# Gated cross-attention and ternary feed-forward layer: four of six bias products issued as 32-row tiles

## What is computed

```python
def bit_linear(x, w, b):                       # x rounded to 255 levels per token, w to -1, 0, 1
    gamma_x = clip(max(abs(x), axis=-1), 1e-05); scale_x = 127.0 / gamma_x
    x_dq = clip(round(x * scale_x), -128, 127) / scale_x
    gamma_w = clip(mean(abs(w)), 1e-05)
    w_dq = clip(round(w / gamma_w), -1, 1) * gamma_w
    return x_dq @ w_dq.T + b
x = x + tanh(g_xattn) * attention(layernorm(x), ctx)
h = layernorm(x)
x = x + tanh(g_ffn) * bit_linear(silu(bit_linear(h, gate_w, gate_b)) * bit_linear(h, val_w, val_b), out_w, out_b)
```

## Time and profile before

| | us |
|---|---|
| median of 3 runs | 773.2 (772.61 to 775.05) |
| profiled execution | 772.76 |
| its span, first to last instruction | 771.0 |
| TensorE products busy | 706.6 |
| VectorE busy | 622.7 |
| ScalarE busy | 535.4 |
| GpSimd busy | 316.9 |

### The profile page before, as it was taken

One profiled execution on the slowest core, in us unless ns is written; L12 is line 12 of the kernel. 1 busy time (PEld: TensorE's weight loads), 2 busy tenths in 40 slices (PEclk: granted clock), 3 DMA queues, 4 the chain that ended last, 5 costly groups with the idle time before them and its releaser, 6 DMA issues.

```text
span 771.0 us, 13495 instructions
## 1 busy us (share of the span) xinstructions
PE 706.6 (92%) x4204; PEld 341.1 (44%) x4253; DVE 622.7 (81%) x1290; ACT 535.4 (69%) x701; POOL 316.9 (41%) x482
## 2 busy tenths in 40 slices
PE   4989755878999999999999999999999999999997
PEld 3434434433544454445444444444444544454443
DVE  6868797697778987798779877987798778778885
ACT  4575778977657956786678856795588657856554
POOL 4310315223554356344643454346444553354440
PEclk9999886989999999999999999999999999999999
DMA  9864426121453354435443354326433542244312
GB/s 324 254 232 124 116 83 212 42 39 45 113 130 67 83 111 105 106 82 109 95 116 82 80 124 90 85 63 129 106 79 81 115 96 62 55 93 86 83 42 69
DMA packets 177386, 81.07 MB, mean 105 GB/s; under 512 B 156595, under 2 KB 156851, under 8 KB 176710
## 3 DMA queue, kind: packets, MB, share of 16 engines
q1 hardware_dynamic: 177350, 80.62, 42.7%
HBM read 38.75 MB, written 10.51 MB: 64 GB/s over the span
## 4 chain that ended last, share of the span: by engine, by line
PE 37%; DVE 33%; issue 10%; ACT 6%; DMA 5%; another core or an unknown queue 5%; POOL 2%; SPq 1%; DVEq 0%; POOLq 0%; ACTq 0%
PE psum L1739 12%; PE psum L1705 11%; PE psum L1730 5%; DVE psum L1227 3%; DVE hmax L1240 2%; DMA arena<-x_both 2%; PE psum L1709 2%; DVE arena L1235 2%; PE psum L1932 2%; ACT arena L921 2%; DVE xmax L1312 2%; DVE stats L1300 2%; DVE arena L1346 2%; DVE stats L1266 2%
## 5 line engine op out<-in xcount | busy, mean ns | idle before, releaser
L1705 PE MATMUL psum<-ternary,xqT 128*128 128x512 f16 x1024 | 259.6, 382 | 3.2 <-DVE xqT L1257 1.1
L1705 PEld LDWEIGHTS psum<-ternary,xqT 128*128 128x128 f16 x1024 | 98.3, 98 | 120.3 <-DVE arena L1232 2.8
L665 POOL TENSOR_TENSOR rstd<-var_e,minus_half 128x1 f32<-128x1 f32 x64 | 39.8, 623 | 211.1 <-DVE var_e L1304 111.1
L1730 PE MATMUL psum<-ternary,arena 128*128 128x512 f16 x496 | 121.7, 379 | 1.5 <-DMA arena<-arena 1.5
L855 ACT ACTIVATE arena<-psum,dequant 128x512 f32<-128x512 f32 x128 | 87.1, 681 | 49.7 <-PE psum L1709 47.4
L1739 PE MATMUL psum<-wo_hi,arena 128*128 128x512 f16 x256 | 82.6, 384 | 0.3
L1240 DVE TENSOR_REDUCE hmax<-arena 128x1 f32<-128x1024 f32 x64 | 77.6, 1213 | 0.8
L1739 PE MATMUL psum<-arena,wq_hi 128*128 128x512 f16 x256 | 76.1, 379 | 1.7 <-DMA arena<-x_both 1.1
L863 ACT ACTIVATE arena<-arena,round_c,hscale 128x1024 f32<-128x1024 f32 x62 | 73.5, 1235 | 1.9 <-DVE hscale L1252 1.9
L895 ACT ACTIVATE arena<-arena,round_c 128x1024 f16<-128x1024 f32 x62 | 70.8, 1142 | 0.3
L1730 PEld LDWEIGHTS psum<-ternary,arena 128*128 128x128 f16 x496 | 46.2, 98 | 54.8 <-issue 3.8
(11 more groups left out here) (213 smaller groups left out, 1302.1 us busy)
## 6 DMA issues: line engine op xcount, KB each, us to landing
arena<-in_x SPq DMA_DIRECT2D x64, 256.0 KB, 2.8
out<-arena SPq DMA_DIRECT2D x31, 256.0 KB, 2.4
arena<-in_L_ffn_gate_w SPq DMA_DIRECT2D x4, 1024.0 KB, 12.9
arena<-in_L_ffn_out_w SPq DMA_DIRECT2D x3, 1024.0 KB, 4.9
ternary<-in_L_ffn_val_w SPq DMA_DIRECT2D x2, 1024.0 KB, 11.9
kcur<-k_scratch SPq DMA_DIRECT2D x56, 32.0 KB, 2.2
arena<-arena SPq DMA_TRANSPOSE x90, 3.1
ternary<-in_ctx SPq DMA_DIRECT2D x1, 1024.0 KB, 5.4
```

What stands on the lines that cost most here:

```text
L1705: ins = M.matmul(ps[:], xqT[:, t % 2, k, :], w[:, k, cols], start=(k == 0), stop=(k == KC - 1 and not biased))
L1730: ins = M.matmul(psO[:], hidT[t % 2][:, k, :], wo2[:, k, :], start=(k == 0), stop=(k == FC - 1))
```

## The change

The first product of a tile's block 0 is now preceded by four products of 32 rows each: rows 0 to 31 of inv_rows and bias_parts into psG[0], rows 32 to 63 into psG[1], rows 64 to 95 into psV[0], rows 96 to 127 into psV[1]. They open the sums of gate and value blocks 0 and 1, and the eight products of those blocks add to them. Gate blocks 2 and 3 keep a full bias product of 128 rows (the three other groups are zero there). Value blocks 2 and 3 get theirs from VectorE, value blocks 0 and 1 no longer do. Ahead of the four, TensorE waits until the readers of block 3 of the tile before are done (not for t = 0). For the four groups the inverse scale's parts are repeated four times, and the biases are stored three times to a larger scratch, so that the rows are read back in five DMAs.

```diff
-        bias_dram = nc.dram_tensor("bias_scratch", [PARTS, 2, F], BF16, kind="Internal").ap()
+        bias_dram = nc.dram_tensor("bias_scratch", [PARTS, PARTS, 2, F], BF16, kind="Internal").ap()
-        bias_parts = sb("bias_parts", [P, F + F // 2], BF16)
+        bias_parts = sb("bias_parts", [P, 3 * CW], BF16)
-        ones_p = sb("ones_p", [P, 2, PARTS])
+        ones_p = sb("ones_p", [P, 2, 2, PARTS])
+        BIAS_ROWS = [(2 * g + h, 0, g, slice(h * CW, (h + 1) * CW)) for g in range(2) for h in range(2)]
+        BIAS_ROWS += [(0, 1, 0, slice(2 * CW, 4 * CW))]
-                    sp.dma_start(valb_b[:, :], bcast(val_b[0:F // 2], F // 2)).then_inc(s_vbias, 16)
+                    sp.dma_start(valb_b[:, :], bcast(val_b[F // 2:], F // 2)).then_inc(s_vbias, 16)
-            sp.dma_start(bias_dram.rearrange("j g (p c) -> p (j g) c", p=P),
-                         bias_cut.rearrange("p j g c -> p (j g) c")).then_inc(s_bst, 16)
+            for r in range(PARTS):
+                sp.dma_start(bias_dram[r].rearrange("j g (p c) -> p (j g) c", p=P),
+                             bias_cut.rearrange("p j g c -> p (j g) c")).then_inc(s_bst, 16)
-            sp.wait_ge(s_bst, 16)
-            for i in range(2 * PARTS):
-                g, j = i // PARTS, i % PARTS
-                n = F // 2 if g else F
-                sp.dma_start(bias_parts[PARTS * i:PARTS * (i + 1), g * F:g * F + n],
-                             bias_dram[j:j + 1, g, F - n:].to_broadcast([PARTS, n])).then_inc(s_brow, 16)
+            sp.wait_ge(s_bst, 16 * PARTS)
+            for r, at, g, cols in BIAS_ROWS:
+                sp.dma_start(bias_parts[GROUP * r:GROUP * r + PARTS * PARTS, at * CW:at * CW + cols.stop - cols.start],
+                             bias_dram[:, :, g, cols].rearrange("r j n -> (r j) n")).then_inc(s_brow, 16)
-                parts = inv_cols[:, t % 2, 0:2 * PARTS * PARTS].rearrange("p (g i j) -> p g i j", g=2, j=PARTS)
+                parts = inv_cols[:, t % 2, :].rearrange("p (g h n) -> p g h n", g=2, h=2)
-                    G.tensor_tensor(parts[:, :, :, j], ones_p[:],
-                                    src.rearrange("p (g a) -> p g a", a=1).to_broadcast([P, 2, PARTS]),
-                                    ALU.mult).then_inc(iv_part.sem, 1)
+                    G.tensor_tensor(parts[:, :, :, PARTS * j:PARTS * (j + 1)], ones_p[:],
+                                    src.rearrange("p (g a n) -> p g a n", a=1, n=1)
+                                    .to_broadcast([P, 2, 2, PARTS]), ALU.mult).then_inc(iv_part.sem, 1)
-                    if n < BIASED_BY_VECTOR:
+                    m = n - (NCH - BIASED_BY_VECTOR)
+                    if m >= 0:
+                    if i == 0 and t:
+                        wait(pe, silu_done, b, m - 1)
+                        wait(pe, hid_ready, b, m - 1)
+                    if i == 0:
+                        for r in range(4):
+                            part = slice(GROUP * r, GROUP * (r + 1))
+                            M.matmul((psG, psV)[r // 2][r % 2][:], inv_rows[part, t % 2, :], bias_parts[part, 0:CW],
+                                     start=True, stop=False)
-                        if m > 2:
+                        if i >= 2:
                             wait(pe, used, b, m - 2)
+                        last_bias = g == 0 and i >= 2
                         for k in range(KC):
-                            biased = g == 0 or i >= BIASED_BY_VECTOR
-                            ins = M.matmul(ps[:], xqT[:, t % 2, k, :], w[:, k, cols], start=(k == 0),
-                                           stop=(k == KC - 1 and not biased))
-                        if biased:
-                            at = (g * F // 2) + i * CW
-                            ins = M.matmul(ps[:], inv_rows[:, t % 2, :], bias_parts[:, at:at + CW],
+                            ins = M.matmul(ps[:], xqT[:, t % 2, k, :], w[:, k, cols], start=(i >= 2 and k == 0),
+                                           stop=(k == KC - 1 and not last_bias))
+                        if last_bias:
+                            ins = M.matmul(ps[:], inv_rows[:, t % 2, :], bias_parts[:, (i - 1) * CW:i * CW],
                                            start=False, stop=True)
```

More of the change, by code:

```diff
@@ L687, in update_inverse @@
                     src = left if j else whole
-                    G.tensor_tensor(parts[:, :, :, j], ones_p[:],
-                                    src.rearrange("p (g a) -> p g a", a=1).to_broadcast([P, 2, PARTS]),
-                                    ALU.mult).then_inc(iv_part.sem, 1)
+                    G.tensor_tensor(parts[:, :, :, PARTS * j:PARTS * (j + 1)], ones_p[:],
+                                    src.rearrange("p (g a n) -> p g a n", a=1, n=1)
+                                    .to_broadcast([P, 2, 2, PARTS]), ALU.mult).then_inc(iv_part.sem, 1)
                     if j < PARTS - 1:
                         wait(pool, iv_part, row, PARTS * t + j + 1)
-                        G.tensor_tensor(left, src, parts[:, :, 0, j], ALU.subtract).then_inc(iv_left.sem, 1)
+                        G.tensor_tensor(left, src, parts[:, :, 0, PARTS * j], ALU.subtract).then_inc(iv_left.sem, 1)
                         wait(pool, iv_left, row, (PARTS - 1) * t + j + 1)
@@ L1223, in hidden @@
                     wait(dve, v_done, b, NCH * t + n + 1)
-                    if n < BIASED_BY_VECTOR:
-                        if not prev and (t, n) == (0, 0):
+                    m = n - (NCH - BIASED_BY_VECTOR)
+                    if m >= 0:
+                        if not prev and (t, m) == (0, 0):
                             dve.wait_ge(s_vbias, 16)
                         V.scalar_tensor_tensor(out=psV[n % 2], in0=psV[n % 2], scalar=dequant[:, t, 1:2],
-                                               in1=valb_b[:, n * CW:(n + 1) * CW],
+                                               in1=valb_b[:, m * CW:(m + 1) * CW],
                                                op0=ALU.mult, op1=ALU.add).then_inc(vb_ready.sem, 1)
-                        wait(dve, vb_ready, b, BIASED_BY_VECTOR * t + n + 1)
+                        wait(dve, vb_ready, b, BIASED_BY_VECTOR * t + m + 1)
                         wait(dve, silu_done, b, NCH * t + n + 1)
@@ L1693, in gate_val @@
                         if t == 0 and not prev:
-                            pe.wait_ge(s_brow, 16 * 2 * PARTS)
+                            pe.wait_ge(s_brow, 16 * len(BIAS_ROWS))
                     if t == 0 and not prev:
```

## The result

The changed kernel takes 769.35 us (median of 8 runs, 768.48 to 770.79) against 772.9 (8 runs, 772.14 to 775.05): ratio 0.995, 95% interval 0.9938 to 0.9962. It is faster, as forecast, and the time lies in the range of 755.0 to 770.0, but 3.6 us were saved and not 14.

A forecast was written before the change was run, and what follows sets the result against it. TensorE was taken to set the pace. Six turns 12.4, row 0 1.9 and the last row 1.1 saved, less 1.5 in setup, made 13.9 us off the 773.2 median: 759.3, bounds 755.1 to 765.1, range 755.0 to 770.0.

The forecast's parts named there:

- The pack: Four 32-row products opening a tile overlap and cost 0.35 us, range 0.22 to 0.41; a tile saves 0.51 where TensorE is last.
- a sign of being wrong: The prediction called itself wrong if, among other signs, the four 32-row products cost over 0.41 us.
- the change of form: On TensorE, changing into the half-width form costs at most 0.09 us, read from the attention's products.
- B: The four 32-row products run one after another without drains, 0.86 us; 3.4 saved, 769.8 us; chance 0.11.
- C: The four run one after another and each change of form drains, 1.19 us a tile; 776.7 us, slower; chance 0.10.
- Rival A: Each change between full and 32-row products drains the array, 0.16 us, twice a tile; 766.2 us; chance 0.17.
- Tile 0: In a turn, TensorE saves 0.51 us and the queries' wait for a transpose gives 0.10: 0.61 together.
- Tile 1: In a turn, gate block 3 ends earlier, and SiLU, a table load and the exponentials follow: 0.30 us saved.
- Tile 2: In a turn, VectorE has two blocks shorter and one longer between the statistics and the scale: 0.70 us saved.
- Tile 3: In a turn, inv_rows stays where it is and TensorE comes forward 0.45 us before meeting it: 0.45 saved.
- Last row: First two tiles save 0.51 us each plus small gaps, 1.1 in all; the last tile's late vector biases cost 0.
- Setup: Three bias stores instead of one delay row 1's x: 1.5 us lost, bounds 0 and 6.0; VectorE's statistics near 52.5.

The follow-up runs named there:

- serial_pack: The changed kernel with all four 32-row products on rows 0 to 31 instead of four groups of rows; 782.51 us, ratio 1.011.
- order_pool: The changed kernel with three of GpSimd's instructions moved (beta add to x, sum of the result, low part of x); 765.12 us, ratio 0.9882.
- pe_only: The changed kernel with VectorE's two biases back in blocks 0 and 1, pack and three stores kept; 769.18 us, ratio 0.9939.
- vector_only: The kernel before with VectorE's value bias moved to blocks 2 and 3, TensorE keeping six full bias products; 775.63 us, ratio 1.0024.
- one_store: The changed kernel with one store of the bias parts instead of three, and 15 small loads instead of five; 768.33 us, ratio 0.9932.
- codes_before: The kernel before with ScalarE making the hidden codes of tile 3 ahead of its SiLU, nothing else; 772.9 us, ratio 0.9996.
- third_silu_first: order_pool with tile 3's low part of x behind GpSimd's second root and, on ScalarE, hidden codes earlier, high part of x later; 762.27 us, 0.9844.
- both_before: The kernel before with order_pool's GpSimd order, tile 3's low part of x behind the first root, its hidden codes ahead of SiLU; 773.37 us.
- pool_before: The kernel before with the GpSimd order of order_pool, nothing else; 778.94 us, ratio 1.0067.

## Why the prediction was wrong

By stretch of the program, forecast and measured in the two profiled executions (771.0 and 767.0):

| stretch | forecast | measured |
|---|---|---|
| until the first tile of row 0 | +1.5 | +0.4 |
| row 0 | -1.9 | -1.6 |
| six turns | -12.4 | -3.1 |
| last row and end | -1.1 | +0.4 |
| sum (before rounding) | -13.9 | -4.0 |

In a turn 1.70 of the 2.06 are missing: 1.02 in tile 2, 0.55 in tile 3, 0.10 in tile 1 and 0.03 in tile 0.

- **The pack: right in mechanism, its size a little off.** Taken as 0.35 within 0.22 to 0.41; 0.43 to 0.47 measured, over the bound that was named as a sign of being wrong. That is 0.08 a tile, about 1.7 us in 21 tiles. Starts overlap, as the products against the values suggested, though in tiles 1 to 3 the four start within 0.01 of each other and not some 0.03 apart, and serial_pack shows that it hangs on different rows. What was put too low is the change of form: 0.09 once, and about 0.10 at each of two changes measured. Rivals B and C are refuted, although B's 769.8 is almost the measured time: the rows and serial_pack's 782.5 speak against it, not the total. Rival A had the right kind of cost, at 0.16 a change instead of 0.10. The Trainium skill, "TensorEngine Tiling (Array Packing)", Key Properties, says that changing the mode drains TensorE. The trace agrees as far as a step of about 0.10 goes at each change (0.20 a tile, where A paid 0.33); that a drain makes the step is not shown.
- **Tile 0: the number right (0.58 of 0.61), by parts that cancel.** The pack gives 1.29 - 0.43 - 0.43 = 0.43 and not 0.51. The queries' wait gives about 0.31 and not 0.10, since it cost twice what its bracket says and goes altogether. And the first product against xqT comes up to 0.15 later behind the pack than in the other tiles, which order_pool hasn't (24.69). pe_only gives 0.65, so the vector side adds nothing here. **Tile 1: right in mechanism**, gate block 3 is what counts: 3 x 0.216 - 0.44 = 0.21, which is what the tile gave; 0.30 used the pack's 0.35.
- **Tile 2: wrong.** The step that failed is the one from "Blocks 0 and 1 become 0.70 shorter each" to a gain of 0.70 for what is queued behind them: VectorE's list was added up with no look at what GpSimd does beside it. Block 1 passes its 0.70 on; block 0 is followed by the new x, which can't end before GpSimd's add plus 0.54. In tile 2 itself the new x is hardly held (0.77), and the chain from the statistics to the scale does get 0.49 shorter (13.36 from start to start instead of 13.85; 0.70 less a few short waits). But the bound ahead of it is hit instead: the statistics start 0.68 later in the tile, and from the reciprocal to tile 3 it takes 0.13 more. 0.68 - 0.49 + 0.13 = +0.32, as measured. order_pool shows the part of the clash: 0.74 back.
- **Tile 3: wrong** at "TensorE may come forward by about 0.45 before it meets" inv_rows. Two things failed. I took only one of the tile's inputs for the next limit and never looked at what DMA brings into its middle: the hidden codes, which arrived at the very moment they were used. And "The sum over a tile is unchanged, so xqT comes no later" is false: from the statistics to xqT it took 466.22 - 452.67 = 13.55 before and 464.01 - 449.72 = 14.29 after, 0.74 more, because block 0's saving is lost to GpSimd and those of blocks 2 and 3 are paid in full. It ate the slack of 0.67 and left a wait that costs 0.13. In order_pool the same stretch takes 13.30 and inv_rows is ready 1.00 ahead of the next tile, so the clash is what made it late. And "Tiles 0 and 3 are TensorE end to end" was not so for tile 3, which had 0.3 in gaps.
- **Last row: wrong sign.** I let the late biases cost nothing. ScalarE now waits 0.91 for the hidden scale of tile 2, and the 16 products behind that tile's transposes wait 1.82, 1.28 before. They start 52.4 into the row instead of 52.1, although the pack saves TensorE 0.43 a tile; vector_only shows the whole stretch 3.1 longer without the pack. In the changed kernel:

```profile
746.88 2.37 ACT L865 ACTIVATE arena<-arena,round_c,hscale 128x1024 f32<-128x1024 f32 x2 [0.91 <-DVE hscale L1255]
...
755.75 3.61 PE L1740 MATMUL psum<-ternary,arena 128*128 128x512 f16 x16 [1.82 <-DMA arena<-arena]
```

- **Setup: the event right** (52.42 for 52.5), its price not: 1.5 taken, 0.4 seen at the first tile, and one_store gives none of it back. Even the 0.4 isn't told apart from nothing: codes_before, whose setup is that of the kernel before, starts its first tile at 129.9 and the kernel before at 131.7.

After GpSimd's order and ScalarE's codes are moved (third_silu_first), the six turns take 470.7 us against 481.0 before, 10.2 less where 12.4 were forecast. Not all of it is the change's: against both_before (480.3) it is 9.6, and the last edit of ScalarE was not run on the kernel before. So the mechanism is worth about three quarters of its forecast, on a kernel that wasn't this one.

Open: why tile 0's pack is up to 0.15 longer in the changed kernel, and what each of the two limits in tile 3 costs alone. third_silu_first's turn is 0.3 above 78.1; its wait for the transfer costs 0.37.

## What to carry to other kernels

When work is moved in front of or away from an instruction, list what runs beside that instruction on other engines before and after; a record that is longer in some places than in others (0.74, 0.85, 1.07) is an instruction that is held already, and shortening what stands ahead of it buys nothing. Before TensorE is credited with a saving, check each input that arrives inside the stretch, transfers above all: two rows with the same distance with and without a wait show a limit that has no slack. Take the price of a wait from the distance of two starts, not from the bracket: here a wait of 0.16 cost 0.33 and one of 0.64 cost 0.80. And judge a theory by its rows and not by its total: a wrong rival matched the time to 0.5 us.

## What the runs showed of the hardware

- VectorE's new x (two f32 inputs in SBUF, one output) and GpSimd's 512-column f32 add don't run side by side: 0.74 us alone, and beside an add it ends 0.54 to 0.57 after the add, in 35 of 35 cases of before and after. The bound (one f32 input, 1024 columns) is held as well: 0.69 alone, two in 2.99, and GpSimd's add beside it takes 1.72 instead of 1.27. Instructions that read PSUM on VectorE keep their 0.75 and 0.69 beside such adds.
- Four 32-row products of 512 columns: 0.33 us from the first to the next full product on four different groups of rows, 0.95 on one group. Each change between full and 32-row products adds about 0.10 to the distance of two starts, so the pack costs 0.43 to 0.47.
- The same order of GpSimd's instructions gives the changed kernel 4 us and costs the kernel before 5 (order_pool and pool_before), in the latter by one transpose that is issued later.
